# Down projection of a mixture of experts: both parts of the weights as one moving operand of 512 columns, one PSUM bank for a tile of rows

## The reference

```python
g = einsum('bsh,ehf->ebsf', x, w_gate)        # H = 256, F = 1024, E = 8
u = einsum('bsh,ehf->ebsf', x, w_up)
h = silu(g) * u
expert_out = einsum('ebsf,efh->ebsh', h, w_down)
out = einsum('ebsh,bse->bsh', expert_out, cw)  # cw: weights of the experts for each row
x = x + out
```

## Time and profile before

| | us |
|---|---|
| time, median of 3 runs (984.3 to 985.77) | 985.31 |
| time of the profiled execution | 985.77 |
| its span, first to last instruction | 984.0 |
| busy: PE / PEld | 971.3 / 927.1 |
| busy: DVE / ACT / POOL | 747.7 / 481.7 / 671.7 |

### The profile page before, as it was taken

The page is one execution under the profiler, slowest core; times in us unless marked ns, Lnnn a source line. Parts: engine busy times, 40 slices in busy tenths (PEclk is TensorE's granted clock), DMA queues, the critical chain, the costliest instruction groups (busy, mean ns, idle before and its releaser), DMA issues.

```text
span 984.0 us, 16545 instructions
## 1 busy us (share of the span) xinstructions
PE 971.3 (99%) x6184; PEld 927.1 (94%) x6184; DVE 747.7 (76%) x1352; ACT 481.7 (49%) x853; POOL 671.7 (68%) x514
## 2 busy tenths in 40 slices
PE   7899999999999999999999999999999999999998
PEld 6899999999999999999999999999999999999998
DVE  5888446877787777887778877778877788777785
ACT  5887544454544444454445444444544453444441
POOL 4699876776767576676757676766767576767642
PEclk9999999999999999999999999999999999999999
DMA  6522140000101001010001010010100010100002
GB/s 175 138 86 78 42 149 22 22 24 21 44 22 43 23 22 43 22 44 23 23 22 44 22 44 23 22 43 22 44 22 23 22 44 23 43 22 23 1 1 76
DMA packets 37889, 40.63 MB, mean 41 GB/s; under 512 B 3185, under 2 KB 35809, under 8 KB 37809
## 3 DMA queue, kind: packets, MB, share of 16 engines
q1 hardware_dynamic: 37808, 39.58, 13.1%
HBM read 35.90 MB, written 3.67 MB: 40 GB/s over the span
## 4 chain that ended last, share of the span: by engine, by line
PE 97%; DMA 1%; DVE 1%; POOL 0%; SPq 0%; issue 0%; ACT 0%; DVEq 0%; ACTq 0%; POOLq 0%
PE ps L268 94%; DMA xsacc<-in_x 1%; PE ps L1517 1%; PE ps L1605 1%; DMA xf<-in_L_xattn_Wk 0%; PE ps L1592 0%; PE ps L1545 0%; PE ps L1562 0%; PE ps L1506 0%; POOL arena L415 0%; PE ps L1611 0%; DVE early L1072 0%; DVE arena L272 0%; POOL xsacc L422 0%; ACT early L634 0%
## 5 line engine op out<-in xcount | busy, mean ns | idle before, releaser
L268 PE MATMUL ps<-arena 128*128 128x256 f32 (+4 forms) x3120 | 414.2, 284 | 1.3 <-DVE arena L1059 1.3
L268 PEld LDWEIGHTS ps<-arena 128*128 128x128 f32 (+2 forms) x3120 | 402.8, 189 | 8.0 <-DVE arena L1059 1.7
L482 POOL TENSOR_TENSOR arena<-shared,arena 128x448 fp32r<-128x448 f32 x196 | 251.2, 1296 | 190.9 <-ACT arena L806 185.3
L268 PE MATMUL ps<-xc_hi,w_hi 128*128 128x448 f32 x904 | 331.8, 367 | 0.0
L268 PE MATMUL ps<-xc_hi,w_lo 128*128 128x448 f32 x904 | 330.2, 365 | 0.0
L268 PE MATMUL ps<-xc_lo,w_hi 128*128 128x448 f32 x904 | 329.8, 365 | 0.0
L799 ACT ACTIVATE shared<-shared 128x448 f32<-128x448 f32 x180 | 101.4, 579 | 191.9 <-DVE shared L1171 124.9
L268 PEld LDWEIGHTS ps<-xc_hi,w_lo 128*128 128x128 f32 x904 | 169.8, 188 | 13.8
L268 PEld LDWEIGHTS ps<-xc_hi,w_hi 128*128 128x128 f32 x904 | 170.5, 189 | 10.3
L268 PEld LDWEIGHTS ps<-xc_lo,w_hi 128*128 128x128 f32 x904 | 170.6, 189 | 10.2
L1165 DVE TENSOR_TENSOR shared<-ps,shared 128x448 f32<-128x448 f32 x60 | 37.5, 624 | 111.2 <-PE ps L268 111.2
(11 more groups left out here) (142 smaller groups left out, 1098.5 us busy)
## 6 DMA issues: line engine op xcount, KB each, us to landing
early<-in_L_ffn_w_down SPq DMA_DIRECT2D x16, 512.0 KB, 4.0
shared<-in_ctx SPq DMA_DIRECT2D x16, 336.0 KB
w_raw<-in_L_ffn_w_gate SPq DMA_DIRECT2D x17, 256.0 KB, 3.0
w_raw<-in_L_ffn_w_up SPq DMA_DIRECT2D x17, 256.0 KB, 3.2
early<-in_L_ffn_w_gate SPq DMA_DIRECT2D x15, 256.0 KB, 2.8
early<-in_L_ffn_w_up SPq DMA_DIRECT2D x15, 256.0 KB, 3.3
x_dram<-xsacc SPq DMA_DIRECT2D x8, 224.0 KB, 3.4
xsacc<-x_dram SPq DMA_DIRECT2D x1, 1792.0 KB, 8.0
```

Source lines behind the costliest of these rows:

```text
L268: ins = nc.tensor.matmul(dst, w, m, start=first and i == 0, stop=last and i == len(passes) - 1, skip_group_check=onto)
L482: nc.gpsimd.tensor_tensor(h[:, 1, j, at:at + TC], tile, h[:, 0, j, at:at + TC].bitcast(fp32), ALU.subtract).then_inc(hid_lo_done, 1)
```

## The change

The high and the low part of a block of down weights now lie side by side (`wd_wide`), 512 columns. A pass with the high hidden values as the loaded operand runs over all 512 and fills a whole bank: columns 0 to 255 get high x high, columns 256 to 511 get high x low. A second pass of 256 columns adds low x high to the first half. So a block takes two passes (512 and 256) in place of three of 256, and a tile of rows takes a bank. VectorE adds each tile in two instructions, the second half of the bank (`add_half`) and the first (`add_rest`), each with the weight per row. Banks 6 and 7 now hold two row tiles at a time, and TensorE waits before tile r (counted over all groups, r = 7g + i) for the second add of tile r - 2. The first four tiles of group 0 and the last tile of the last group keep the passes of 256 columns; the row that comes last before the end uses bank 0, and the last group uses seven banks.

In the order of work, tile 2 goes behind the up products 1, 6, 5 of the odd quad. On VectorE the adds of tile 4 go ahead of `gate_u2` of the even quad, those of 5 and 6 between `up_u2` and `gate_u3_c22`; in the odd quad those of 0 and 1 stay behind `gate_u2` in the order half 0, half 1, rest 0, rest 1, those of 2 go between `up_u2` and `gate_u3_c22`, and those of 3 ahead of `up_u3_c22`.

```diff
-        wd = arena[:, 2 * HS:2 * HS + WD].rearrange("p (l t d) -> p l t d", l=2, t=FT)
+        wd_wide = arena[:, 2 * HS:2 * HS + WD].rearrange("p (t n) -> p t n", t=FT)
+        wd = wd_wide.rearrange("p t (l d) -> p l t d", l=2)
...
-        ps_r = [ps[:, 6 + i // 2 % 2, i % 2 * D:(i % 2 + 1) * D] for i in range(RT)]
+        ps_first = [ps[:, 6 + i // 2, i % 2 * D:(i % 2 + 1) * D] for i in range(NARROW)]
+        ps_rows = [ps[:, 6 + i, :] for i in range(2)]
+        ps_before = ps[:, 0, :]
+        ps_end = [ps[:, i, :] for i in (3, 4, 5, 6, 1, 2, 7)]
...
+            def add_half(g, i, src, made=None):
+                ve.wait_ge(row_ready, RT * g + (made or i + 1))
+                add(g, i, src[:, D:2 * D]).then_inc(acc_half, 1)
+
+            def add_rest(g, i, src, made=None):
+                ve.wait_ge(acc_half, RT * g + (made or i + 1) - NARROW)
+                add(g, i, src[:, 0:D]).then_inc(acc_done, 1)
...
                 g, odd = n // FPAIRS - 1, n % FPAIRS
+                if not odd:
+                    add_rows(g - 1, 4)
                 gate_u2(n)
                 if odd:
-                    add_rows(g, 0, ps_r[0])
-                    add_rows(g, 1, ps_r[1])
+                    for i in (0, 1):
+                        add_half(g, i, ps_rows[(RT * g + i) % 2])
+                    for i in (0, 1):
+                        add_rest(g, i, ps_rows[(RT * g + i) % 2])
+                up_u2(n)
+                if odd:
+                    add_rows(g, 2)
                 else:
-                    add_rows(g - 1, 4, ps_r[4])
-                    add_rows(g - 1, 5, ps_r[5])
-                up_u2(n)
+                    add_rows(g - 1, 5)
+                    add_rows(g - 1, 6)
                 gate_u3_c22(n)
                 if odd:
-                    add_rows(g, 2, ps_r[2])
-                    add_rows(g, 3, ps_r[3])
+                    add_rows(g, 3)
                 up_u3_c22(n)
-                if not odd:
-                    add_rows(g - 1, 6, ps_r[6])
...
+            def wide(dst, g, i, steps, first=True, last=True):
+                toks = slice(i * P, (i + 1) * P)
+                for n, (fp, j) in enumerate(steps):
+                    h, t = hs[(FPAIRS * g + fp) % HSLOTS], 2 * fp + 1 - j
+                    end = last and n == len(steps) - 1
+                    if end:
+                        nc.tensor.matmul(dst[:, 0:D], h[:, 1, j, toks], wd[:, 0, t, :], start=False, stop=False)
+                    ins = nc.tensor.matmul(dst, h[:, 0, j, toks], wd_wide[:, t, :], start=first and n == 0, stop=end)
+                    if not end:
+                        ins = nc.tensor.matmul(dst[:, 0:D], h[:, 1, j, toks], wd[:, 0, t, :], start=False, stop=False)
+                return ins
...
+                else:
+                    pe.wait_ge(acc_done, 2 if r == NARROW else r - 1)
+                    wide(ps_rows[r % 2], g, i, STEPS).then_inc(row_ready, 1)
...
                 gate_1_6_5(n)
+                if n % FPAIRS == 0:
+                    down(g - 1, 5)
+                up_1_6_5(n)
                 if n % FPAIRS:
                     down(g, 2)
                 else:
-                    down(g - 1, 5)
-                up_1_6_5(n)
-                if n % FPAIRS == 0:
                     down(g - 1, 6)
```

More of the change, by code:

```diff
@@ L59, in xattn_ffn_kernel @@
     PROD = {p: i + 1 for i, p in enumerate((1, 6, 5, 2, 7, 4, 3))}
+    NARROW = 4
     U2_SUM, U3_SUM, C22_SUM, C21_SUM, C12_SUM = range(1, 6)
@@ L200, in xattn_ffn_kernel @@
         u_a, u_x, u_y = [ps[:, 3 + i, 0:TC] for i in range(3)]
-        ps_r = [ps[:, 6 + i // 2 % 2, i % 2 * D:(i % 2 + 1) * D] for i in range(RT)]
-        ps_end = ps_r[0:4] + [ps[:, i // 2, i % 2 * D:(i % 2 + 1) * D] for i in range(RT - 4)]
+        ps_first = [ps[:, 6 + i // 2, i % 2 * D:(i % 2 + 1) * D] for i in range(NARROW)]
+        ps_rows = [ps[:, 6 + i, :] for i in range(2)]
+        ps_before = ps[:, 0, :]
+        ps_end = [ps[:, i, :] for i in (3, 4, 5, 6, 1, 2, 7)]
         x_parts = [sem(f"x_part{i}") for i in range(4)]
@@ L245, in xattn_ffn_kernel @@
         act_done, hid_done, hid_hi_done, hid_lo_done = sem("act_done"), sem("hid_done"), sem("hid_hi_done"), sem("hid_lo_done")
-        row_ready, acc_done, stored = sem("row_ready"), sem("acc_done"), sem("stored")
+        row_ready, acc_half, acc_done, stored = sem("row_ready"), sem("acc_half"), sem("acc_done"), sem("stored")
         PARTS = {"first": (A11, slice(0, 3, 2), 2), "second": (A21, slice(1, 4, 2), 2), "s13": (S1, slice(4, 6), 2),
@@ L1223, in add_plain_rows, with add, add_rows @@
                     ve.wait_ge(acc_in, DMA)
[L1224 to L1232, removed]
+                ve.wait_ge(row_ready, (i // 2 + 1) * 2)
+                add(0, i, ps_first[i]).then_inc(acc_done, 1)
+            def add(g, i, src):
+                e, tile = g // (HALVES * CP), g % CP * RT + i
+                return nc.vector.scalar_tensor_tensor(acc[:, tile, :], src, cw[:, tile, e:e + 1], acc[:, tile, :], ALU.mult, ALU.add)
+            def add_half(g, i, src, made=None):
[4 more added lines that the diff above has]
+                add(g, i, src[:, 0:D]).then_inc(acc_done, 1)
+            def add_rows(g, i, src=None):
+                bank = ps_rows[(RT * g + i) % 2] if src is None else src
+                add_half(g, i, bank)
+                add_rest(g, i, bank)
             def from_top():
@@ L1456, in _ @@
                 quad(n)
[L1457 to L1460, removed]
+            for i in (4, 5):
+                add_rows(GROUPS - 2, i)
+            add_rows(GROUPS - 2, 6, ps_before)
+            g = GROUPS - 1
+            for n, i in enumerate((4, 5, 0, 1, 2, 3)):
+                add_half(g, i, ps_end[i], n + 1)
+                add_rest(g, i, ps_end[i], n + 1)
+            ve.wait_ge(row_ready, RT * GROUPS)
+            add(g, RT - 1, ps_end[RT - 1][:, 0:D]).then_inc(acc_done, 1)
         @block.tensor
@@ L1701, in row_passes @@
                                                            wd[:, 0, 2 * fp + 1 - j, :], wd[:, 1, 2 * fp + 1 - j, :])]
+            def wide(dst, g, i, steps, first=True, last=True):
[9 more added lines that the diff above has]
+                return ins
+            STEPS = [(fp, j) for fp in range(FPAIRS) for j in range(2)]
             def down(g, i):
@@ L1715, in down @@
                     pe.wait_ge(logits_done, CP)
-                if i % 2 == 0:
-                    at_least(pe, acc_done, RT * g + i - 2 if i > 2 else RT * g - 1 if i == 0 else RT * g)
-                accumulate(ps_r[i], [t for fp in range(FPAIRS) for t in row_passes(g, i, fp)]).then_inc(row_ready, 1)
+                r = RT * g + i
+                if r < NARROW:
+                    accumulate(ps_first[i], [t for fp in range(FPAIRS) for t in row_passes(g, i, fp)]).then_inc(row_ready, 1)
+                elif r == RT * (GROUPS - 1) - 1:
+                    pe.wait_ge(act_done, 4 * (QUADS - 1) + HID11)
+                    wide(ps_before, g, i, STEPS).then_inc(row_ready, 1)
+                else:
+                    pe.wait_ge(acc_done, 2 if r == NARROW else r - 1)
+                    wide(ps_rows[r % 2], g, i, STEPS).then_inc(row_ready, 1)
             pe.wait_ge(lg_cleared, 1)
@@ L1912, in _ @@
             last = 4 * (QUADS - 1)
[L1914 to L1921, removed]
             pe.wait_ge(wd_done, SETS)
             pe.wait_ge(hid_lo_done, last)
-            pe.wait_ge(act_done, last + HID11)
             pe.wait_ge(gate_sum, 5 * (QUADS - PLAIN))
-            for i in range(4, RT):
-                earlier(i)
+            for i in (4, 5):
+                wide(ps_end[i], g, i, STEPS[0:2], last=False)
+            pe.wait_ge(hid_done, last + HID11)
+            wide(ps_end[0], g, 0, STEPS[0:2], last=False)
             pe.wait_ge(hid_lo_done, 4 * QUADS)
[L1931 to L1939, removed]
+            for i in (4, 5, 0):
+                wide(ps_end[i], g, i, STEPS[2:4], first=False).then_inc(row_ready, 1)
+            pe.wait_ge(up_sum, 5 * (QUADS - PLAIN))
+            for i in (1, 2):
+                wide(ps_end[i], g, i, STEPS).then_inc(row_ready, 1)
+            for i, count in ((3, RT * g - 2), (6, RT * g - 1)):
+                pe.wait_ge(acc_done, count)
+                if i < RT - 1:
+                    wide(ps_end[i], g, i, STEPS).then_inc(row_ready, 1)
+                else:
+                    accumulate(ps_end[i][:, 0:D], [t for fp in range(FPAIRS) for t in row_passes(g, i, fp)]).then_inc(row_ready, 1)
 _INS = ['x', 'ctx_1024', 'L0_xattn_Wq', 'L0_xattn_bq', 'L0_xattn_Wk', 'L0_xattn_bk', 'L0_xattn_Wv', 'L0_xattn_bv',
```

## The result

The change makes the kernel slower: 994.19 us median of 4 runs (994.1 to 994.75) against 984.89 for the kernel before (4 runs, 984.3 to 985.77), ratio 1.0095 with a 95% interval of 1.0077 to 1.0112. The profiled execution spans 992.4 us, before 984.0.

What follows compares the result with a forecast made beforehand. TensorE's queue was taken to bound the kernel: -8.2 us from wide passes and +1.4, +11.8 and +1.9 of waits gave +6.9, on 985.77 992.7, less 0.46 for the median 992.2 us; own range 989 to 995, with rivals 979.5 to 998.

Steps and rivals of the forecast that it cites:

- The wait: TensorE at tile 2 of each odd quad waits for VectorE's `rest` add of tile 0: 1.4 + 11.8 + 1.9 us.
- the 14 pairs of turn 2: Pairs of even quads 6, 10, ..., 58: `gate_u2` at O + 2.53, tile 2 waits 0.84 us, 11.8 us in all.
- the other 15: Pairs whose even quad had turn 0: `gate_u2` at O + 1.78, tile 2 waits 0.09 us, 1.4 us in all.
- the first pair: Quad 5, `gate_u2` behind `sums_2_4` at O + 3.60: tile 2's wait over at 5.54, 1.9 us, once.
- The step that `hidden22` would be held by the third sum: VectorE's `hidden22` in turn 2 starts within GpSimd's third sum, ends at 519.87 instead of 519.93; `gate_u2` gains 0.06, not 0.39.
- the sums don't hold it: Rival, 12%: GpSimd's sums don't hold up `hidden22`, `gate_u2` gains some 0.4, those 14 pairs wait 0.5; 987.4 us.
- `hidden21` gets in first: Rival, 14%: VectorE's `hidden21` starts before GpSimd's low part, takes 0.61, and the 11.8 us of waits go; 980.4 us.
- Two old passes took 0.2396, so a block gains 0.0094: TensorE's row tiles: a 512 pass costs 0.2302 us against 0.2396 for two of 256; 876 blocks give -8.2 us.
- the line through 256 and 448: TensorE's pass cost extended linearly from 256 columns (0.1198 us) and 448 (0.2026) to 512: 0.2302 us.
- the chances of a slower kernel: Forecast, no gain from wide passes, more waits than counted, and half of the sums rival: 0.72 in all.
- The other new waits: TensorE's waits of tile r for tile r - 2, other than tile 2, have a microsecond or more in hand.
- the added 0.8 us ahead of it: Tile 4's adds on VectorE delay the even quad's `gate_u2` by 0.8 us; TensorE needs it only 3 us later.

Runs made afterwards that it cites:

- the kernel with tile 2 later: Against the changed kernel, tile 2's matmuls go behind gate products 2 and 7, tile 3's behind up 2 and 7, adds one place back; 980.62 us.
- tile 2 later and three passes: Against the changed kernel, tiles 2 and 3 go later as do their adds, and each block takes three passes of 256 columns; 985.63 us.

## Why the prediction was right

The forecast was 992.2 us, +6.9; it came +9.3 by the medians and +8.4 by the two profiled executions. The sign did not hang on luck: the waits were put 0.8 us too high and the gain 3.6, and neither miss is near what would have turned the sum.

**The wait** was right by place, mechanism and size. For the 14 pairs of turn 2 the prediction had `gate_u2` at 2.53 and 0.84 us of wait; the trace has 2.51 and 0.81. For the other 15 it had 1.78 and 0.09; the trace has 1.75 and 0.06 to 0.07. In the first pair tile 2 starts 1.77 late, 1.9 with its restart, as forecast. The sum, 14 x 0.81 + 15 x 0.07 + 1.9 = 14.3 us, stands against 15.1, and the kernel with tile 2 later, which keeps some 0.7 us of it in the first pair, takes 13.6 us off.

**Why half of the pairs are worse** was shown, not only argued: with GpSimd's sums moved they lost their excess, 10.5 us. The step that `hidden22` would be held by the third sum came out (0.95 for 0.61), and with it the rivals fell by which the sums don't hold it or `hidden21` gets in first. The SBUF — State Buffer page of the Trainium skill (SBUF: two separate sides) has this as a lock that the first instruction keeps; the runs agree: 1.21 and 1.58 us against 0.61, and a wait that GpSimd's order alone decides.

**The term that was mis-sized** is "Two old passes took 0.2396, so a block gains 0.0094", -8.2 us. Averaged over the 28 pairs from the start of quad 7 to that of quad 63, a pair takes 27.087 us before, 27.087 with tile 2 later and three passes, and 26.940 with tile 2 later and wide passes. That is 0.147 for 28 blocks, 0.0052 a block, in all -4.6 us. The tiles by themselves gain a little more: two narrow ones in a row take 2.873 us on average and two wide ones 2.829, 0.0055 a block; a single one takes 1.435 before and 1.409 with tile 2 later, 0.0063. The two pairs of kernels with and without wide passes agree: 5.0 us with tile 2 later, and 3.1 in the changed order, where the earlier arrival gives some 1.3 us back as longer waits. What was wrong with the line through 256 and 448 stays open; it is a matter of 0.004 us in 0.23, which decides over almost half of the gain.

The Trainium skill (TensorE: Matmul & The Clock Gate, Back-to-back issue gap) has N/2.4 + 2.5 ns, and calls it the gap of an isolated matmul; by it a block would gain 2.5 ns, as an estimate 2.2 us in all. The measured gain lies between it and the line, and the measured distances, 120 ns for 256 columns and 234 ns for 512 (the average in the kernel with tile 2 later), lie 11 and 18 ns above it.

**Sum with the measured terms:** -4.6 + 14.3 = +9.7 us. In the scheduled quads, which hold 210 of the 219 wide tiles, it is -4.4 + 14.3 = +9.9, where the profile has +9.8. Ahead of them the profiled execution is 0.8 us shorter than the one before. That looks like scatter: in the ten profiles of this case, the scheduled quads start between 153.8 and 154.8 us. Behind them it is 0.6 us shorter: 0.2 are the wide passes, and 0.4 lie behind VectorE's last add, which ends 2.2 us before the end of the span, and 2.6 in the kernel before.

**Two slips in the prediction's sums** touch neither the forecast nor its range: the first pair is counted with 1.94 us where the others have 1.96, and the chances of a slower kernel, as they are listed, come to 0.74 and not 0.72, which leaves 0.05 for no change.

**The other waits** were rightly put at nothing: no wait for an add stands in the trace but those of tile 2. `gate_u2` of the even quad, the added 0.8 us ahead of it, and the tiles 3 to 6 stayed hidden. VectorE had gone to 86% busy without being the bound anywhere else.

## What to carry to other kernels

This change saved the bounding engine half a percent and gave the engine beside it more work, and it was decided at the first place where the two meet. So mark the release of each buffer on the time axis of the waiting engine, instruction by instruction, before shares of busy time are looked at. When buffers in flight are halved, put the instruction that frees the next buffer first in its queue: here the adds ahead of one independent instruction, or the waiting tile two products later, turned 994.2 us into 980.7 and 980.6, faster than both kernels. And look on a third engine for what delays the second: here its order decided whether a gain of 0.39 us in VectorE's queue arrived (`gate_u2` from 2.10 to 1.75 us) or was lost (from 2.52 to 2.51).

## What the runs showed of the hardware

- Two VectorE instructions with both inputs in SBUF that meet GpSimd's low parts one behind the other go turn by turn with them: 1.21 and 1.58 us in place of 0.61, each ending some 0.5 us after the GpSimd instruction it waited for. Even the short sums of 256 columns hold VectorE (0.95). The row adds, with one input in PSUM, kept their 0.48 us.
- TensorE's wait costs more than the profile's idle time of it: 0.55 in the bracket, 0.81 by starts, of which 0.10 lies between the first and the second pass behind the wait (0.34 in place of 0.24).
- A pass less with the same columns is worth 5 to 6 ns here, about 5% of the 120 ns of a pass of 256.
- An add that needs the add just before it starts 0.52 us after it, an independent one 0.39 (the four adds take 1.91 us in the order half 0, rest 0, half 1, rest 1, and 1.65 with both halves first). Such an add waits for `acc_half` and also reads what the one before wrote; which of the two costs the 0.13 us, no run tells apart.
